# The repeated src row of two graph convolutions, loaded as bytes or as bf16 for every other buffer

## The reference

```
h = tanh(gcn_conv(x, W1, b1)); h = tanh(gcn_conv(h, W2, b2))
gcn_conv: hw = h @ W; msg = hw[row] * norm; agg = segment_sum(msg, col) + b
```

## Time and profile before

| | |
|---|---|
| median of 3 runs | 9425.87 us (9421.83 to 9431.37) |
| the profiled execution | 9435.26 us, span 9433.5 us |
| first expansion stage | about 6556 to 7185 us |
| second expansion stage | about 7992 to 8620 us |
| DVE busy over the span | 85% |
| DMA read, written | 684.63 MB, 285.30 MB |

### The profile page before, as it was taken

The page is one execution under the profiler, slowest core; times in us unless marked ns, Lnnn a source line. Parts: engine busy times, 40 slices in busy tenths (PEclk is TensorE's granted clock), DMA queues, the critical chain, the costliest instruction groups (busy, mean ns, idle before and its releaser), DMA issues.

```text
span 9433.5 us, 304022 instructions
## 1 busy us (share of the span) xinstructions
PE 5903.3 (63%) x115811; PEld 5165.9 (55%) x116055; DVE 7971.5 (85%) x12544; ACT 2918.1 (31%) x7087; POOL 3247.3 (34%) x2803
## 2 busy tenths in 40 slices
PE   7960004888788888888888884444554444555443
PEld 6740004888676777777777773443554444554443
DVE  6759982444699999999999998888999998999998
ACT  5630001222355545445444541001552000553000
POOL 5410015777311111111111115663003775003775
PEclk9999999999766666666666665555555555555555
DMA  3000004999522222222222222224564224664224
GB/s 43 12 13 2 0 17 157 333 334 332 182 86 86 87 86 87 87 86 86 86 86 86 86 84 60 62 62 66 179 179 121 62 62 60 180 178 127 62 62 53
DMA packets 524393, 971.22 MB, mean 103 GB/s; under 512 B 134852, under 2 KB 349060, under 8 KB 507156
## 3 DMA queue, kind: packets, MB, share of 16 engines
q1 hardware_dynamic: 376532, 717.71, 23.1%
q0 software_dynamic: 127872, 252.39, 12.6%
q10 hardware_dynamic: 19904, 0.13, 0.2%
HBM read 684.63 MB, written 285.30 MB: 103 GB/s over the span
## 4 chain that ended last, share of the span: by engine, by line
DVE 41%; issue 19%; PE 11%; DVEq 11%; DMA 10%; ACTq 4%; ACT 2%; POOL 2%; SPq 0%; POOLq 0%
DVEq L1452 8%; DVE lane_hotb L1448 6%; DMA val_rows<-val_out 5%; PE ps L826 4%; PE ps L883 4%; DMA dw_in<-dst_wide 3%; DVE acc L1457 3%; ACTq L786 3%; DVE keys L1227 2%; DVE keys L1228 2%; DVE prod L1493 2%; DVE prod L1496 2%; DVE low L1506 2%; DVE whole L1504 2%; DVE prod L1501 2%
## 5 line engine op out<-in xcount | busy, mean ns | idle before, releaser
L1448 DVE TENSOR_TENSOR lane_hotb<-rel_all,iota_b 128x1024 bf16<-128x1024 bf16 x2928 | 1832.8, 686 | 95.6 <-PE ps L985 72.2
L985 PE MATMUL ps<-got,lane_hotb 128*128 128x48 bf16 x23424 | 1067.6, 215 | 1295.7 <-DVE lane_hotb L1448 1267.9
L985 PEld LDWEIGHTS ps<-got,lane_hotb 128*128 128x128 bf16 x23424 | 973.6, 118 | 1389.6 <-issue 1364.1
L538 POOL DMA_INDIRECT got<-val_rows,dst_idx x976 | 1120.2, 1148 | 1764.8 <-DMA val_rows<-val_out 1359.3
L538 POOL DMA_INDIRECT xs_buf<-xd_rows,src_idx x488 | 585.0, 1199 | 2630.7 <-DVE whole L1504 2490.0
L1605 DVE TENSOR_SCALAR wide_hotb<-sw_inb,slot_id 128x2048 bf16<-128x2048 uint8 x976 | 1194.3, 1282 | 55.3 <-DMA sw_inb<-src_byte 46.0
L960 PEld LDWEIGHTS ps<-w2c,hid 128*128 128x128 f32 x7808 | 1091.3, 223 | 14.7
L960 PE MATMUL ps<-w2c,hid 128*128 128x32 f32 x7808 | 1062.7, 300 | 35.8 <-issue 28.2
L1019 PE MATMUL ps<-wide_tabb,wide_hotb 128*128 128x48 bf16 x15616 | 711.8, 215 | 558.1 <-DVE wide_hotb L1605 289.4
L1019 PEld LDWEIGHTS ps<-wide_tabb,wide_hotb 128*128 128x128 bf16 x15616 | 649.2, 118 | 620.8 <-issue 525.8
L883 PE MATMUL ps<-row_tab,dst_hot 128*128 128x32 bf16 x31488 | 816.4, 178 | 111.8 <-DVE dst_hot L1402 93.3
(11 more groups left out here) (350 smaller groups left out, 9244.2 us busy)
## 6 DMA issues: line engine op xcount, KB each, us to landing
dw_in<-dst_wide SPq DMA_DIRECT2D x128, 1312.0 KB
xd_rows<-xd_out SPq DMA_DIRECT2D x128, 984.0 KB
sw_in<-src_wide SPq DMA_DIRECT2D x244, 512.0 KB, 4.8
sw_inb<-src_byte SPq DMA_DIRECT2D x488, 256.0 KB, 3.9
val_rows<-val_out SPq DMA_DIRECT2D x488, 192.0 KB, 2.5
msg_rows<-msg_out SPq DMA_DIRECT2D x244, 200.0 KB, 2.2
got<-val_rows,dst_idx POOLq DMA_INDIRECT x976
src_key<-chunk_keys,src_idx POOLq DMA_INDIRECT x488
```

Of the source, the lines that this page charges most:

```text
L538: return pool.indirect_dma_start(out=into, out_offset=None, in_=table, in_offset=bass.IndirectOffsetOnAxis(index, 0))
L985: last = mm(ps_sum[q % 2 * 2 + h][:, half * 3 * D:(half + 1) * 3 * D], lane_hot2[s][:, h * CH + t, half * P:(half + 1) * P], got[q % 4][:, ...
L1448: return v.tensor_tensor(to.rearrange("p t (j k) -> p t j k", k=2), rel.unsqueeze(2).to_broadcast(shape), iota_b[:, :].rearrange("p (j k) ...
```

## The change

The second and fourth of the four row buffers stay uint8 and take `src_byte`; the first and third become bf16, twice as large, and take `src_wide`. No other instruction, wait or order is altered.

```
-        sw_in2 = [sb(f"sw_inb{k}", [P, 2 * CH * P], U8, of=pf) for k in range(4)]
+        sw_in2 = [sb(f"sw_inb{k}", [P, 2 * CH * P], U8 if k % 2 else BF16, of=pf) for k in range(4)]
...
                 for q in range(4):
-                    load_src(sw_in2[q], sw2_got[l][q], q, src_byte_v)
+                    load_src(sw_in2[q], sw2_got[l][q], q, src_byte_v if q % 2 else src_wide_v)
...
                         sp.wait_ge(whot2_ready[l], i * 4 + (q + 1))
-                        load_src(sw_in2[q], sw2_got[l][q], i * 4 + (q + 4), src_byte_v)
+                        load_src(sw_in2[q], sw2_got[l][q], i * 4 + (q + 4), src_byte_v if q % 2 else src_wide_v)
```

## The result

The changed kernel takes 9515.32 us (median of 6 runs), the kernel before 9425.64 us in the same comparison. The ratio is 1.0095 with a 95% interval of 1.0081 to 1.0109: slower by 90 us, as forecast in sign, and twice the size. One of the six executions took 14693.68 us and is left out of the ratio; the median of the other five is 9513.37 us. 9515 is close to the number of rival 4, 9516. The two profiled executions are 78.1 us apart (spans 9511.6 and 9433.5).

What follows compares the result with a forecast made beforehand. The bound was taken as a three-group loop of store, load, next store's landing and ACT's pass. Terms +50 - 7 + 2 = +45 us on 9435.3 gave 9480, 9471 on the median's scale, rounded to 9468; range 9365 to 9545.

Steps and rivals of the forecast that it cites:

- rival 4: Expansion stage: a bf16 load lands 0.9 us later by contention, ACT at its floor; +92 us, 9516; chance 0.10.
- three-group loop: Expansion stage: store, next load's landing, next store's landing, ACT's pass, store; 7.73 us for three groups, 2.577 each.
- b: Expansion stage: time from an even group's store to the next odd one's; 2.38 us, raised to 2.43.
- ACT's pass of 2.43: Expansion stage: an ACT pass without a store wait took 2.43 us, so b is at least about that.
- DVE's 252 us counted at nothing: Expansion stages: faster bf16 comparisons save DVE 0.52 us a group, 252 us over 488 groups, counted as nothing in the loop.
- The load's price: Expansion stages: a 512 KB load lands 0.6 us later than 256 KB; 2.68 us a group, +50 us.
- DVE's relief: Expansion stages: fewer late hand-overs from DVE, so ACT waits less for TensorE; -7 us, ends 0 and -20.
- The collects: Start of the collects: first gathers may wait for two larger first loads, 1.2 us, twice; +2 us.
- From the profile to the median: Whole kernel: the runs' median is 9.4 us below the profiled execution, moving the forecast from 9480 to 9471.
- 1: ACT's wait for the store of g-2: landings do not depend on the load; -49 us, 9377; faster rivals together 0.30, this 0.19.
- 2: Expansion stages: DVE was the bound; -68 to -171 us, about 9300; chance 0.11.
- 3: Expansion stages: no change, load costs 0.3 us or less more and DVE's relief is 20 us; 9430; chance 0.17.

Runs made afterwards that it cites:

- the two kernels with a mean of 512 KB: Kernel before with four bf16 row buffers, 512 KB loads: ratio 1.0156; kernel before on bytes with 768 and 256 KB loads in turns: 1.0158.
- the fastest kernel: Changed kernel with four output buffers and each load issued one group earlier, ahead of the store it followed: 9638.06 us, ratio 0.9743 to the kernel before.

## Why the prediction was right in the mechanism and wrong in the size

**The bound.** Right, though one of its two supports was weak. The absence of DVE from 60 us of the chain proved little: over the whole first stage DVE held 5.0% of it, and with four output buffers a DVE that never rested was missing from 200 us. What carried it was the pace. The three-group loop gave 2.577 us a group for the kernel before (2.572 measured). With 1.0 us for the load it gives 16.46 / 6 = 2.743 for the changed kernel (2.740 and, in the second stage, 2.724), 2.743 for large byte loads (2.747), 2.91 for the two kernels with a mean of 512 KB (2.905 and 2.928). The same equations give b = 7.73 - 2 x 2.743 = 2.24 for the changed kernel; in its first stage b was 2.26 on average. It was under 2.43 in 66 of 120 cases, so ACT's pass of 2.43, which the prediction took for a floor, was none.

**DVE's 252 us counted at nothing.** Right: 1.0002 for the fast comparison alone. DVE at 95% busy was not the bound.

**The load's price, the step that failed.** "I take 0.6: the expansion stage has no gathers and keeps the engines 62% busy." It measured 1.0, 4.9 against 3.9 us. The term of the loop was therefore +0.167 us a group instead of +0.103, +81 us instead of +50, and the sum would have been +76 against the 78.1 between the two profiled executions. The 0.6 was taken from the first of four loads, which has nothing ahead of it (3.6 against 4.1), and from the spacing of landings. In the stage every load has a 192 KB store 0.6 to 0.95 us ahead of it in its queue. The row that had such a neighbour was the earlier trace rows, 4.8 us or +0.9, from the stage of the edge messages. SP's timeline there, in the trace of the kernel before (`msg_rows` is a store of 200 KB):

```profile
4513.65 0.40 SPq L471 DMA_DIRECT2D msg_rows<-msg_out  x1
4514.31 0.34 SPq L466 DMA_DIRECT2D sw_in<-src_wide  x1
```

I put its +0.9 down to the gathers; the same 4.9 appears in a stage without any. The +1.1 of the earlier trace rows, 3.8 against 4.9, is no clean witness, since there the transfer ahead doubles too. That the store ahead is the reason is in part argued. For it speaks the kernel with GpSimd's stores, in which the store ahead is mostly 2 us off or more and 512 KB landed in 3.9 us; but its stores were also in another queue. What the runs show without doubt is the slope of about 1.0 us per 256 KB in the kernels where SP issues both.

**DVE's relief.** 7 us were taken. The chain shows -0.08 us a round of two groups in one stretch, the fast comparison alone -0.03 us a group, some 15 us; its time shows none. It lies within the ends given, 0 and -20.

**The collects.** +2 us taken; they changed by 2 us in all. That agrees by luck as far as is known: it is +2.5 in one collect and about nothing in the others, and no run shows a first gather waiting for a larger load.

**From the profile to the median.** The sum stood on an execution that was 9.4 us above the median, and I subtracted this, which left the forecast's rise as the traces' difference. The profiled execution of after was not above its median, so 12 of the 90 us between the medians are not in the traces' difference. Of the 47 us between the forecast's rise of 42 and the measured 90, 31 are the load's price, 12 are these, 3 are the rounding from 9471 to 9468, which went the wrong way, and some 2 are left.

**What was to be seen.** Comparisons of 747 and 1281 ns, DVE near 72%, DMA share near 0.7, byte loads near 3.9: all seen. Of the chain DVE held nothing from 6700 to 6760 us. The loads of `src_wide` landed in 4.9 us, not in 4.4 to 4.6, and the stores were 2.74 us apart, not 2.68. The landings of stores did not fall into two classes by parity. In the first stage the even groups' stores, behind a bf16 load, took 2.99 us on average and the odd ones' 2.92, where 0.4 to 0.6 was forecast between them. The distance between stores adjusts itself: an even group's store followed 3.22 us behind the store before it, an odd one's 2.26, and a store issued later after its load waits less.

**The rivals.** 1 and 2 fall with the two halves measured apart, 3 with the result. Against 1 stand the landings too: one and the same 192 KB store took 2.0 to 4.3 us within the first stage, by where it stood behind its load. 4 had the right number, 9516, by nearly the right rise in landing (0.9) and for two wrong reasons: gathers that the stage does not have, and ACT's floor of 2.43. Without the floor its own sum is (15.46 + 0.9) / 6 = 2.727, +73 us. Its hit on the number is partly luck.

## What to carry to other kernels

An engine that is 95% busy can still be the follower: divide the stage by its groups, compare with the engine's own pace, and look for the loop that makes up the difference. In a loop that passes through a DMA's completion, price a larger transfer by a row in which the same neighbours are in the queue ahead of it, not by an isolated one. Do not clear an engine because the chain of waits leaves it out; compare paces, or speed it up alone. A trade of DMA bytes for engine time pays only after the landings are off the loop; here two more output buffers and an earlier load turned the same edit from +0.95% into part of a -2.6%.

## What the runs showed of the hardware that was not expected

Of the three chips of the experiments the second and third needed 9909 and 9893 us for the kernel that takes 9428 on the first. The stage that expands the dst rows moved 243 to 249 GB/s there in place of 333. DVE waited 777 us for its loads of 1312 KB, and 512 us on the first chip. Landings in the expansion stages were within some tenths of a microsecond of the first chip's (GB/s in 40 slices, of the kernel with 768 KB loads):

```profile
GB/s 38 11 3 14 0 16 128 249 245 243 247 147 85 86 88 85 85 87 87 85 85 87 87 85 65 62 63 92 245 247 175 62 62 75 243 247 189 62 61 53
```

TensorE's granted clock in the first expansion stage rose from 0.50 to 0.53 when the groups came more slowly and TensorE was busy 52% of the time in place of 57%; in the fastest kernel it was 0.62 at 64% busy. With bytes and four output buffers it was 0.50 at 61%. Values between 0.50 and 1 are means of a stretch over the two levels, 1.2 and 2.4 GHz. I have no explanation that these numbers fit.
